# Routed FFN ahead of its first expert block: half items, the block table first, and the facts of odd tiles multiplied on GpSimd

## The chip, the cores and the metric

The kernel runs on one core of a Trainium2 chip. The metric is the device time of one execution in microseconds (us). The engines are TensorE (PE, matmuls; PEld is its weight load), VectorE (DVE), ScalarE (ACT), GpSimd (POOL) and SyncE (SP, which here only issues DMAs). Each runs its own list of instructions in order and waits on semaphores for the others. SBUF is the on-chip memory, PSUM the memory that matmuls write.

## The reference

Eight layers work on one sequence of 1024 tokens with 512 features in float32. Two of them, the sixth (L1f) and the eighth (L1g), are a routed FFN, and they alone are touched:

```
scores = sigmoid(x @ gate_w.T) + bias              # 16 experts
topk_w, topk_idx = top_k(scores, 4)                # 4 experts for each token
topk_w = topk_w / (sum(topk_w) + 1e-20)
g, u = x @ Wg[e].T, x @ Wu[e].T                    # for each expert e
out = sum over e of  cw[t, e] * (silu(g) * u) @ Wd[e].T
out = out + (silu(x @ Sg.T) * (x @ Su.T)) @ Sd.T   # the shared expert, for every token
```

The inner width is 256, for the shared expert too.

## The kernel before

`routed_ffn` computes the shared expert for all tokens, and the routed experts only for the tokens that chose them. The 4096 picks (1024 tokens, 4 each) are sorted by expert into NB = 47 blocks of 128 slots, and the blocks run one after the other.

**The head, ahead of the first block.** PE turns the normalised rows, computes the router's logits, and then the shared expert in four items. Item m is one 128-column chunk of the inner width for one half of the tokens: first its gate part (u = 0), then its up part (u = 1), 12 matmuls each. Its sums stand in PSUM pair m % 2. ACT takes the Silu of the gate part, DVE multiplies it by the up part into `z_all` (`item(m)` of DVE). PE's item m waits for DVE's item m - 2, since they use the same pair. Items and routing are interleaved in a written order: item 0, the turned scores, item 1, the ranks, items 2 and 3, `told`, the shared expert's down projection. No scheduler moves anything.

**The routing on DVE** is one long list of small instructions: score, top 8, expert indices (`hit`), `chosen`, DVE's item 0, the weights in three bf16 parts (`facts`), the places after PE's `rank`, then `slot_f`, the slot of each pick. From it come `offset_f` (slot within a block) and `at_block` (which of the 47 blocks), and for each of the 8 token tiles two products: `at_offset` (128 x 4 x 128, bf16; it lies in the tile `shared_raw`, under whose name the trace shows it) and `fact` (128 x 4 x 5 x 47 = 940 a lane, bf16). Then comes the table `block_i` of the blocks' experts, and DVE's item 1. PE sums at_offset times fact over 32 picks into `told`, and DVE makes `token` and `weight` from it: which token and weight stand in each slot.

**The down projection of the shared expert** (L1892) is 8 tiles of tokens, each 2 matmuls of float32 (4 records in the trace) into one of three PSUM banks; DVE adds each into x (L2080, `added`). It is queued on PE behind `told`.

**The blocks.** POOL gathers the rows of block b by `token` with an indirect DMA (L1754), PE turns them (`turn_block`; blocks 0 and 1 also wait for all 8 `added`), ACT and DVE split rows (L1795, L1979) and expert weights (L1788, L1972 `weights_low`) into a high and a low part, and PE multiplies (L1916 to L1918, L1939). DVE scales the result and POOL scatters it with an adding DMA. SP loads weights; its loads of experts 3 and up stand behind the stores of x after `added`, as all of SP's work is in order.

Of the kernel before, what the change touches and what calls it, by code (L numbers as in the profile page):

```python
# [6 lines left out]
ALU = mybir.AluOpType  # L7
# [1579 lines left out]
def weight_set(b):  # L1587

    return (b + 1) % 2


def pair_set(b, p):

    return (2 * (b + 1) + p) % PAIRS


def routed_ffn(nc, g, d, name, sums_dram):
    with stage(nc, name) as (sb, sem), ExitStack() as before_blocks:
# [56 lines left out]
        at_offset_ready, fact_ready, told_ready = sem("at_offset_ready"), sem("fact_ready"), sem("told_ready")  # L1655
# [20 lines left out]
        with nc.Block() as block:  # L1676
# [49 lines left out]
            def _(pool):  # L1726
# [30 lines left out]

                pool.wait_ge(g.padded, 64)
# [73 lines left out]
            def _(pe):  # L1832
# [13 lines left out]
                def item(m):  # L1846
# [4 lines left out]
                    for u in range(2):  # L1851
                        cols = slice(u * INNER + c * P, u * INNER + (c + 1) * P)
                        toks = slice(h * HALF, (h + 1) * HALF)
                        for k in range(KC):
                            mm = product(pe, g.pair[m % 2][:, u * HALF:(u + 1) * HALF], wh[:, pair_set(-1, k // 2), k % 2, cols],
                                         wl[:, pair_set(-1, k // 2), k % 2, cols], xh[:, k, toks], xl[:, k, toks], k == 0, k == KC - 1)
                    mm.then_inc(items_ready, 1)

                item(0)
# [5 lines left out]
                item(1)  # L1865
# [9 lines left out]
                item(2)  # L1875
                item(3)
                told_ps = g.bank(7)[:, 0:FACTS * NB]
                for t in range(NT):
                    pe.wait_ge(at_offset_ready, t + 1)
                    pe.wait_ge(fact_ready, t + 1)  # L1880
                    for i in range(t * TOPK, (t + 1) * TOPK):
                        mm = pe.matmul(told_ps, at_offset[:, i, :], fact[:, i, :, :], start=i == 0, stop=i == PICKS - 1)
                mm.then_inc(told_ready, 1)
                pe.wait_ge(rank_read, 1)
                pe.wait_ge(wd_loaded[weight_set(-1)], 16)
                for t in range(NT):
# [7 lines left out]
                    mm.then_inc(out_ready, 1)  # L1894

# [59 lines left out]
            def _(dve):  # L1955
# [31 lines left out]

                weights_low(-1, 0, None)
# [26 lines left out]
                with nc.allow_low_precision("zeros and ones"):  # L2015
# [30 lines left out]
                then(dve.tensor_copy(slot[:, :], slot_f[:, :]))  # L2046
                then(dve.tensor_scalar(offset[:, :], slot[:, :], P - 1, None, ALU.bitwise_and))
                then(dve.tensor_copy(offset_f[:, :], offset[:, :]))
                then(dve.tensor_tensor(first_slot[:, :], slot_f[:, :], offset_f[:, :], ALU.subtract))
                then(dve.tensor_tensor(at_block[:, :, :], first_slot[:, :].unsqueeze(2).to_broadcast([P, PICKS, NB]),  # L2050
                                       block_no[:, :].unsqueeze(1).to_broadcast([P, PICKS, NB]), ALU.is_equal))
                for t in range(NT):
                    picks, shape = slice(t * TOPK, (t + 1) * TOPK), [P, TOPK, FACTS, NB]
                    dve.tensor_tensor(at_offset[:, picks, :], offset_f[:, picks].unsqueeze(2).to_broadcast([P, TOPK, P]),
                                      in_block[:, :].unsqueeze(1).to_broadcast([P, TOPK, P]), ALU.is_equal)                        .then_inc(at_offset_ready, 1)
# [20 lines left out]
                for m in range(2, ITEMS):  # L2076
                    item(m)
# [146 lines left out]
```

## Time and profile before

| what | us |
|---|---|
| median of 3 runs | 2844.99 |
| lowest and highest run | 2842.21 and 2853.66 |
| the profiled execution, its own time | 2838.49 |
| its span from first to last instruction | 2836.7 |
| PE busy | 2586.0 (91%) |
| DVE busy | 1917.8 (68%) |
| ACT busy | 1494.7 (53%) |
| POOL busy | 823.0 (29%) |

The rows further down are of the profiled execution, and their times count from the start of its span. The granted clock of TensorE has two levels, 1.00 in a row (2.4 GHz) and 0.50 (1.2 GHz). L1g's head stands from 2461 to 2546 us, and L1f's, 768 us earlier, is alike to some tenths of a us.

### The profile page before, as it was taken

How to read it: one execution, taken by the hardware profiler on the slowest of the kernel's cores; microseconds unless marked ns; L12 is line 12 of the kernel's file. 1: busy time of each engine (PE TensorE's matmuls, PEld its weight loads, DVE VectorE, ACT ScalarE, POOL GpSimd, SP SyncE). 2: the span in 40 equal slices, each digit the busy share in tenths (PEclk: the TensorE clock that was granted, in tenths of full speed). 3: DMA queues.
4: the chain of work that ended last, by engine and by line, in shares of the span. 5: the costliest groups of instructions: out<-in, count | busy, mean ns of one | idle time of the engine just before them, and what ended most of it. 6: DMA issues, size and time to landing. Idle time of an engine off the chain costs nothing. (4 is left out here: it accounts for less than half of the span.)

```text
span 2836.7 us, 42839 instructions
## 1 busy us (share of the span) xinstructions
PE 2586.0 (91%) x14886; PEld 1777.5 (63%) x14886; DVE 1917.8 (68%) x3382; ACT 1494.7 (53%) x2528; POOL 823.0 (29%) x777
## 2 busy tenths in 40 slices
PE   7899988878999999999999987899788999868995
PEld 5444434646888888888888864566454444345663
DVE  6877724454777677777777676677578776356774
ACT  5677731314555555555555542466456777315663
POOL 1200001024344353434344320355312000003553
PEclk9899998988999999999999997999988999889998
DMA  4000000010000000000000012988810000229888
GB/s 154 1 1 2 1 18 20 18 38 23 16 23 23 16 27 16 23 23 27 16 23 20 16 35 91 325 217 202 201 58 1 1 1 2 97 75 329 202 199 206
DMA packets 68194, 197.48 MB, mean 70 GB/s; under 512 B 9040, under 2 KB 9936, under 8 KB 62608
## 3 DMA queue, kind: packets, MB, share of 16 engines
q1 hardware_dynamic: 46928, 145.44, 15.1%
q0 software_dynamic: 21056, 49.30, 9.2%
q8 instruction: 125, 2.05, 0.3%
q14 instruction: 85, 0.70, 0.1%
HBM read 154.33 MB, written 40.37 MB: 69 GB/s over the span
## 5 line engine op out<-in xcount | busy, mean ns | idle before, releaser
L1399 ACT ACTIVATE L1a_ph<-single 128x512 fp32r<-128x512 f32 (+3 forms) x384 | 174.4, 490 | 179.9 <-PE single L1486 179.2
L1540 DVE TENSOR_TENSOR L1a_pl<-single,L1a_ph 128x512 fp32r<-128x512 f32 (+3 forms) x384 | 199.2, 548 | 52.8 <-ACT L1a_ph L1399 52.1
L765 DVE TENSOR_REDUCE L0a_least<-single 128x1 f32<-128x512 f32 (+3 forms) x304 | 191.9, 660 | 57.0 <-PE single L587 30.7
L765 DVE TENSOR_REDUCE L1b_least<-single 128x1 f32<-128x512 f32 (+3 forms) x304 | 191.6, 660 | 55.7 <-PE single L587 29.9
L1556 DVE SCALAR_TENSOR_TENSOR x<-single,L1a_rinv,x 128x512 f32<-128x512 f32 x256 | 189.2, 744 | 58.5 <-PE single L1150 58.2
L1390 ACT ACTIVATE L1a_probs<-pair,L1a_least 128x128 f32<-128x128 f32 (+7 forms) x256 | 190.1, 744 | 71.6 <-DVE L1a_least L1534 70.2
L1534 DVE TENSOR_REDUCE L1a_least<-pair 128x1 f32<-128x128 f32 (+7 forms) x256 | 190.5, 749 | 43.2 <-PE pair L1475 42.6
L1367 POOL TENSOR_TENSOR L1a_swapped<-L1a_swapped,L1a_sin 128x512 f32<-128x512 f32 x80 | 129.3, 1617 | 304.5 <-ACT L1a_swapped L1431 304.5
L475 ACT ACTIVATE L0a_probsT<-pair 128x896 f32<-128x896 f32 (+2 forms) x192 | 149.0, 811 | 70.4 <-PE pair L607 47.8
L475 ACT ACTIVATE L1b_probsT<-pair 128x896 f32<-128x896 f32 (+2 forms) x192 | 149.0, 811 | 69.5 <-PE pair L607 46.9
L1486 PE MATMUL single<-ident,L1a_probs 128*128 128x128 f32 x1152 | 169.0, 274 | 1.4 <-ACT L1a_probs L1390 1.4
L1148 PE MATMUL single<-L1a_xh,L1a_wh 128*128 128x512 f32 x384 | 160.4, 418 | 6.0 <-POOL L1a_wl L1356 4.6
L1373 POOL TENSOR_TENSOR L1a_ql<-L1a_lin,L1a_qh 128x512 fp32r<-128x512 f32 x64 | 85.6, 1338 | 235.1 <-DVE L1a_qh L1578 235.1
L1149 PE MATMUL single<-L1a_xl,L1a_wh 128*128 128x512 f32 x384 | 152.3, 397 | 0.0
L1150 PE MATMUL single<-L1a_xh,L1a_wl 128*128 128x512 f32 x384 | 152.2, 396 | 0.0
L1972 DVE TENSOR_TENSOR L1g_wl<-L1g_store,L1g_wh 128x1024 fp32r<-128x1024 f32 x94 | 111.1, 1222 | 60.2 <-ACT L1g_wh L1788 59.0
L1972 DVE TENSOR_TENSOR L1f_wl<-L1f_store,L1f_wh 128x1024 fp32r<-128x1024 f32 x94 | 111.1, 1222 | 59.5 <-ACT L1f_wh L1788 58.5
L1148 PE MATMUL pair<-L1a_kh,L1a_qh 128*128 128x512 f32 (+3 forms) x384 | 140.8, 367 | 7.0 <-POOL L1a_ql L1373 5.7
L1486 PEld LDWEIGHTS single<-ident,L1a_probs 128*128 128x128 f32 x1152 | 130.0, 141 | 13.2 <-ACT L1a_probs L1390 1.7
L1149 PE MATMUL pair<-L1a_kl,L1a_qh 128*128 128x512 f32 (+3 forms) x384 | 133.0, 346 | 0.0
L1150 PE MATMUL pair<-L1a_kh,L1a_ql 128*128 128x512 f32 (+3 forms) x384 | 133.0, 346 | 0.0
L1150 PE MATMUL single<-L1a_ph,L1a_vl 128*128 128x512 f32 (+3 forms) x384 | 132.6, 345 | 0.0
(517 smaller groups left out, 7020.4 us busy)
## 6 DMA issues: line engine op xcount, KB each, us to landing
L1f_wd<-in_L1f_w SPq DMA_DIRECT2D x48, 512.0 KB, 4.4
L1g_wd<-in_L1f_w SPq DMA_DIRECT2D x48, 512.0 KB, 4.4
L1a_raw<-in_L1a_w SPq DMA_DIRECT2D x80, 256.0 KB, 2.6
L1f_store<-in_L1f_w SPq DMA_DIRECT2D x16, 1024.0 KB, 8.1
L1g_store<-in_L1f_w SPq DMA_DIRECT2D x16, 1024.0 KB, 8.3
sum<-L0a_pad_row SPq DMA_DIRECT2D x2, 2304.0 KB, 16.5
sum<-x SPq DMA_DIRECT2D x16, 256.0 KB, 3.0
x<-sum SPq DMA_DIRECT2D x16, 256.0 KB, 5.1
```

The lines of the kernel that those rows point to most:

```text
L475: act.activation(a.probsT[:, i % 2, j, 0:w], g.pair[n % 2][:, 0:w], ACT.Exp, scale=-1.0)\
L765: dve.tensor_reduce(a.least[:, part, qt, first:first + heads], g.bank(BANK16["F", kv, f])[:, 0:heads * w].rearrange("p (j k) -> p j k", j= ...
L1148: pe.matmul(out, wh, xh, start=start, stop=False)
L1149: pe.matmul(out, wh, xl, start=False, stop=False)
L1150: return pe.matmul(out, wl, xh, start=False, stop=stop)
L1390: act.activation(probs[:, u % 2, 0:n], g.pair[u % 2][:, 0:n], ACT.Exp, bias=least[:, u % 4:u % 4 + 1], scale=-1.0, accum_out=rsum[:, h % 2 ...
L1399: act.activation(p_tile(ph, u, i), turned_bank(u, i), ACT.Copy).then_inc(p_high, 1)
L1486: mm = pe.transpose(g.bank(4 + b % 2)[:, k * P:(k + 1) * P], probs[:, u % 2, kt * P:(kt + 1) * P], g.ident[:, :])
L1534: dve.tensor_reduce(least[:, u % 4:u % 4 + 1], g.pair[u % 2][:, 0:(u % NT + 1) * P], AX_X, ALU.min)\
L1540: dve.tensor_tensor(p_tile(pl, u, i), turned_bank(u, i), p_tile(ph, u, i).bitcast(F32), ALU.subtract)\
L1556: dve.scalar_tensor_tensor(out=g.x[:, t, :], in0=aux_bank(("O", h, t)), scalar=rinv[:, h % 2, t:t + 1], in1=g.x[:, t, :], op0=ALU.mult, op ...
L1972: dve.tensor_tensor(wl[:, s, :, :], src, wh[:, s, :, :].bitcast(F32), ALU.subtract).then_inc(w_split, 1)
```

## The change

PE does the items in halves (`item(m, u)`): the turned scores stand behind the first half of item 0 and not behind the whole of it, and the ranks behind the first half of item 1. The down projection (`shared_down`) is cut in three: tiles 0 to 2 ahead of `told`, tiles 3 to 5 behind `told`'s tiles 5, 6 and 7, and tiles 6 and 7 at the end. DVE does item 1 and the table ahead of `slot`, items 2 and 3 between the tiles' products, and the adds of tiles 0 to 2 among them too; its first two `weights_low` move in between the last adds. The `fact` products of tiles 1, 3, 5 and 7 are made by POOL, in the same shape, with a semaphore of their own.

```diff
@@ POOL
+                pool.wait_ge(at_block_ready, 1)
+                for t in range(1, NT, 2):
+                    picks, shape = slice(t * TOPK, (t + 1) * TOPK), [P, TOPK, FACTS, NB]
+                    pool.tensor_tensor(fact[:, picks, :, :], at_block[:, picks, :].unsqueeze(2).to_broadcast(shape),
+                                       facts[:, picks, :].unsqueeze(3).to_broadcast(shape), ALU.mult)\
+                        .then_inc(fact_ready[1], 1)
                 pool.wait_ge(g.padded, 64)
@@ PE
-                item(0)
+                item(0, 0)
                 for t in range(NT):
...
                 mm.then_inc(score_turned, 1)
-                item(1)
+                item(0, 1)
+                item(1, 0)
...
                 mm.then_inc(rank_ready, 1)
-                item(2)
-                item(3)
+                item(1, 1)
+                for m in range(2, ITEMS):
+                    for u in range(2):
+                        item(m, u)
...
+                for t in range(EARLY):
+                    shared_down(t)
+                told_ps = g.bank(7)[:, 0:FACTS * NB]
+                for t in range(NT):
+                    pe.wait_ge(at_offset_ready, t + 1)
+                    pe.wait_ge(fact_ready[t % 2], t // 2 + 1)
+                    for i in range(t * TOPK, (t + 1) * TOPK):
+                        mm = pe.matmul(told_ps, at_offset[:, i, :], fact[:, i, :, :], start=i == 0, stop=i == PICKS - 1)
+                    if t == NT - 1:
+                        mm.then_inc(told_ready, 1)
+                    if t >= NT - EARLY:
+                        shared_down(t - NT + 2 * EARLY)
+                for t in range(2 * EARLY, NT):
+                    shared_down(t)
@@ DVE
+                item(1)
...
-                then(dve.tensor_tensor(at_block[:, :, :], first_slot[:, :].unsqueeze(2).to_broadcast([P, PICKS, NB]),
-                                       block_no[:, :].unsqueeze(1).to_broadcast([P, PICKS, NB]), ALU.is_equal))
+                dve.tensor_tensor(at_block[:, :, :], first_slot[:, :].unsqueeze(2).to_broadcast([P, PICKS, NB]),
+                                  block_no[:, :].unsqueeze(1).to_broadcast([P, PICKS, NB]), ALU.is_equal)\
+                    .then_inc(at_block_ready, 1)
+                dve.wait_ge(at_block_ready, 1)
+                for t in range(NT):
...
+                    if t % 2 == 0:
+                        dve.tensor_tensor(fact[:, picks, :, :], at_block[:, picks, :].unsqueeze(2).to_broadcast(shape),
+                                          facts[:, picks, :].unsqueeze(3).to_broadcast(shape), ALU.mult)\
+                            .then_inc(fact_ready[0], 1)
+                    if t in (0, 2):
+                        item(2 + t // 2)
+                    if NT - 1 - EARLY <= t < NT - 1:
+                        add_shared(t - NT + 1 + EARLY)
...
-                for m in range(2, ITEMS):
-                    item(m)
-                for t in range(NT):
-                    dve.wait_ge(out_ready, t + 1)
-                    dve.tensor_tensor(g.x[:, t, :], g.bank(4 + t % 3), g.x[:, t, :], ALU.add).then_inc(added, 1)
+                dve.wait_ge(table_ready, 1)
+                experts = [expert_of(b) for b in range(2)]
+                for t in range(EARLY, NT - 2):
+                    add_shared(t)
+                for i in range(2):
+                    weights_low(0, i, experts[0])
+                    add_shared(NT - 2 + i)
...
-                weights_low(0, 0, experts[0])
-                weights_low(0, 1, experts[0])
```

The order of DVE's instructions before, from the slots' sum to the table (`shared_raw` is at_offset; the pair of rows L2054 and L2056 stands eight times):

```order
L2045 TENSOR_REDUCE L1f_slot_f<-L1f_part 128x32
L2046 CAST L1f_slot<-L1f_slot_f 128x32
L2047 TENSOR_SCALAR L1f_offset<-L1f_slot 128x32
L2048 CAST L1f_offset_f<-L1f_offset 128x32
L2049 TENSOR_TENSOR L1f_first_slot<-L1f_slot_f,L1f_offset_f 128x32
L2050 TENSOR_TENSOR L1f_at_block<-L1f_first_slot,L1f_block_no 128x1504
L2054 TENSOR_TENSOR L1f_shared_raw<-L1f_offset_f,L1f_in_block 128x512
L2056 TENSOR_TENSOR L1f_fact<-L1f_at_block,L1f_facts 128x940
```

and behind the last of the eight pairs, the table and item 1:

```order
L2054 TENSOR_TENSOR L1f_shared_raw<-L1f_offset_f,L1f_in_block 128x512
L2056 TENSOR_TENSOR L1f_fact<-L1f_at_block,L1f_facts 128x940
L2059 SCALAR_TENSOR_TENSOR L1f_begun<-L1f_start,L1f_block_no 128x752
L2062 TENSOR_REDUCE L1f_block_e<-L1f_begun 128x47
L2063 TENSOR_SCALAR L1f_block_e<-L1f_block_e 128x47
L2064 CAST L1f_block_i<-L1f_block_e 128x47
L1985 TENSOR_TENSOR L1f_z_all<-L1f_gate,pair 128x512
```

DVE's instructions after, behind the slots' sum, item 1 and the table (L2005 is `item`, L2010 an add into x, L2088 at_offset, L2091 fact):

```order
L2082 TENSOR_TENSOR L1f_at_block<-L1f_first_slot,L1f_block_no 128x1504
L2088 TENSOR_TENSOR L1f_shared_raw<-L1f_offset_f,L1f_in_block 128x512
L2091 TENSOR_TENSOR L1f_fact<-L1f_at_block,L1f_facts 128x940
L2005 TENSOR_TENSOR L1f_z_all<-L1f_gate,pair 128x512
L2088 TENSOR_TENSOR L1f_shared_raw<-L1f_offset_f,L1f_in_block 128x512 x2
L2091 TENSOR_TENSOR L1f_fact<-L1f_at_block,L1f_facts 128x940
L2005 TENSOR_TENSOR L1f_z_all<-L1f_gate,pair 128x512
L2088 TENSOR_TENSOR L1f_shared_raw<-L1f_offset_f,L1f_in_block 128x512 x2
L2091 TENSOR_TENSOR L1f_fact<-L1f_at_block,L1f_facts 128x940
L2010 TENSOR_TENSOR x<-single,x 128x512
L2088 TENSOR_TENSOR L1f_shared_raw<-L1f_offset_f,L1f_in_block 128x512
L2010 TENSOR_TENSOR x<-single,x 128x512
```

Four facts are gone from DVE, and items and adds stand between what is left. PE before, behind the last matmul of item 3 (L1882 is told, L1892 the down projection, L1903 the turned rows of blocks 0 and 1):

```order
L1149 MATMUL pair<-L1f_xl,L1f_wh 128x512
L1150 MATMUL pair<-L1f_xh,L1f_wl 128x512
L1882 MATMUL single<-L1f_fact,L1f_shared_raw 128x235 x32
L1892 MATMUL single<-L1f_wd,L1f_z_all 128x512 x16
L1903 MATMUL single<-ident,L1f_xn 128x128 x8
```

and after (L1897 is the down projection, L1908 told, L1923 the turned rows):

```order
L1150 MATMUL pair<-L1f_xh,L1f_wl 128x512
L1897 MATMUL single<-L1f_wd,L1f_z_all 128x512 x6
L1908 MATMUL single<-L1f_fact,L1f_shared_raw 128x235 x24
L1897 MATMUL single<-L1f_wd,L1f_z_all 128x512 x2
L1908 MATMUL single<-L1f_fact,L1f_shared_raw 128x235 x4
L1897 MATMUL single<-L1f_wd,L1f_z_all 128x512 x2
L1908 MATMUL single<-L1f_fact,L1f_shared_raw 128x235 x4
L1897 MATMUL single<-L1f_wd,L1f_z_all 128x512 x6
L1923 MATMUL single<-ident,L1f_xn 128x128 x8
```

Ten of the 16 matmuls of the down projection now stand ahead of the last piece of told.

## Rows read from the trace of the kernel before

**Rows 1.** Waits from 1709 to 1802 us (L1f), one row.

```profile
PE pair L1148 <- DVE L1f_z_all L1985: 17.8, 1, 17.8
```

**Rows 2.** Timeline of PE in L1g's head: start, us, instruction, idle before.

```profile
2484.83 0.40 PE L1148 MATMUL pair<-L1g_xh,L1g_wh 128*128 128x512 f32 x1
...
2490.44 0.67 PE L1863 MATMUL single<-ident,L1g_sigT 16*128 16x16 f32 x8
...
2520.55 0.77 PE L1148 MATMUL pair<-L1g_xh,L1g_wh 128*128 128x512 f32 x1 [17.77 <-DVE L1g_z_all L1985]
...
2528.30 3.48 PE L1882 MATMUL single<-L1g_fact,L1g_shared_raw 128*128 128x235 bf16 x32
2531.62 13.90 PE L1892 MATMUL single<-L1g_wd,L1g_z_all 128*128 128x512 f32 x32
2546.40 1.06 PE L1903 MATMUL single<-ident,L1g_xn 128*128 128x128 f32 x8 [0.88 <-DVE x L2080]
2550.54 0.79 PE L1916 MATMUL pair<-L1g_wh,L1g_bh 128*128 128x512 f32 x1 [3.08 <-DVE L1g_bl L1979]
```

**Rows 3.** Timeline of DVE in L1g's head, the same columns.

```profile
2491.14 0.29 DVE L2001 TENSOR_TENSOR L1g_score<-single,L1g_gb 128x128 f32<-128x128 f32 x1 [9.00 <-PE single L1863]
...
2502.50 1.72 DVE L2050 TENSOR_TENSOR L1g_at_block<-L1g_first_slot,L1g_block_no 128x1504 bf16<-128x1504 f32 x1
2504.26 0.69 DVE L2054 TENSOR_TENSOR L1g_shared_raw<-L1g_offset_f,L1g_in_block 128x512 bf16<-128x512 bf16 x1
2504.87 1.13 DVE L2056 TENSOR_TENSOR L1g_fact<-L1g_at_block,L1g_facts 128x940 bf16<-128x940 bf16 x1
...
2517.47 0.93 DVE L2059 SCALAR_TENSOR_TENSOR L1g_begun<-L1g_start,L1g_block_no 128x752 f32<-128x752 f32 x1
...
2519.73 0.68 DVE L1985 TENSOR_TENSOR L1g_z_all<-L1g_gate,pair 128x512 f32<-128x512 f32 x1
2531.82 0.40 DVE L2067 COPY L1g_told<-single 128x235 f32<-128x235 f32 x1 [11.41 <-PE single L1882]
...
2533.57 0.21 DVE L2075 TENSOR_TENSOR L1g_weight<-L1g_weight,L1g_told 128x47 f32<-128x47 f32 x1
...
2547.52 2.36 DVE L1972 TENSOR_TENSOR L1g_wl<-L1g_store,L1g_wh 128x1024 fp32r<-128x1024 f32 x2 [1.27 <-issue]
```

**Rows 4.** Timeline of ACT, the first block's rows.

```profile
2547.06 0.60 ACT L1795 ACTIVATE L1g_bh<-single 128x512 fp32r<-128x512 f32 x1 [15.36 <-PE single L1903]
```

**Rows 5.** Timeline of POOL: the first gather is issued.

```profile
2534.28 1.02 POOL L1754 DMA_INDIRECT L1g_xn<-rows,L1g_token  x1 [70.56 <-DVE L1g_token L2073]
```

**Rows 6.** DMA issues from 2534.2 to 2535.5 us: count, us to landing.

```profile
L1g_xn<-rows,L1g_token POOLq DMA_INDIRECT x1, 3.6
```

**Rows 7.** Busy us by stretch: PE, PEld, DVE, ACT, POOL, granted clock, DMA share, GB/s.

```profile
2504.70:2520.50 15.80, 0.00 (x0) 0.00 (x0) 15.60 (x21) 0.00 (x0) 0.00 (x0) 0.50 0.00 0
...
2550.50:2555.90 5.40, 5.36 (x13) 4.09 (x14) 2.77 (x3) 1.06 (x1) 0.21 (x1) 0.50 1.01 416
```

**Rows 8.** Timeline of POOL and of DVE around 764 us (attention, L1a).

```profile
762.90 1.29 POOL L1356 TENSOR_TENSOR L1a_wl<-L1a_raw,L1a_wh 128x512 fp32r<-128x512 f32 x1
764.15 1.75 POOL L1367 TENSOR_TENSOR L1a_swapped<-L1a_swapped,L1a_sin 128x512 f32<-128x512 f32 x1
...
764.67 1.78 DVE L1574 TENSOR_TENSOR L1a_lin<-L1a_lin,L1a_swapped 128x512 f32<-128x512 f32 x1
```

**Rows 9.** Two DVE lines, whole trace: count, ns min/median/max, first and last start.

```profile
L1574 DVE TENSOR_TENSOR L1a_lin<-L1a_lin,L1a_swapped x80: 675/681/1782, 649.3 to 1660.7; 128x512 f32<-128x512 f32 x80
...
L1540 DVE TENSOR_TENSOR L1a_pl<-single,L1a_ph x384: 272/617/692, 667.7 to 1680.8; 128x512 fp32r<-128x512 f32 x128, 128x128 fp32r<-128x128 f32 x32, 128x384 fp32r<-128x384 f32 x32
```

**Rows 10.** Timeline of POOL around 56 us: its operand `stack` is bf16.

```profile
56.08 1.40 POOL L412 TENSOR_TENSOR L0a_rest<-L0a_rc,L0a_stack 128x640 f32<-128x640 f32 x1 [6.68 <-ACT L0a_stack L493]
```

**Rows 11.** POOL's groups by shape: count, busy us, mean ns, idle before.

```profile
L435 POOL TENSOR_TENSOR L1b_parts<-L1b_most_rest,L1b_parts 128x16 bf16<-128x16 f32 x16 | 4.3, 271 | 1.3
```

**Rows 12.** Busy us by stretch, as rows 7, of the early blocks.

```profile
2562.00:2625.00 63.00, 55.38 (x232) 36.90 (x232) 42.08 (x53) 35.15 (x53) 29.09 (x21) 1.00 0.98 319
```

More of the change, by code:

```diff
@@ L1850, in item @@
                         pe.wait_ge(z_ready, m - 1)
[L1851 to L1857, printed above, removed]
-                item(0)
+                    cols = slice(u * INNER + c * P, u * INNER + (c + 1) * P)
+                    toks = slice(h * HALF, (h + 1) * HALF)
+                    for k in range(KC):
+                        mm = product(pe, g.pair[m % 2][:, u * HALF:(u + 1) * HALF], wh[:, pair_set(-1, k // 2), k % 2, cols],
+                                     wl[:, pair_set(-1, k // 2), k % 2, cols], xh[:, k, toks], xl[:, k, toks], k == 0, k == KC - 1)
+                    if u:
+                        mm.then_inc(items_ready, 1)
+                item(0, 0)
                 for t in range(NT):
@@ L1874, in _, with shared_down @@
                 mm.then_inc(rank_ready, 1)
-                item(2)
-                item(3)
-                told_ps = g.bank(7)[:, 0:FACTS * NB]
-                for t in range(NT):
[L1879 to L1886, printed above, removed]
+                item(1, 1)
+                for m in range(2, ITEMS):
+                    for u in range(2):
+                        item(m, u)
+                def shared_down(t):
+                    if t == 0:
+                        pe.wait_ge(rank_read, 1)
+                        pe.wait_ge(wd_loaded[weight_set(-1)], 16)
                     if t % BLK == 0:
@@ L2045, in _ @@
                 then(dve.tensor_reduce(slot_f[:, :], part[:, :, :, :].rearrange("p t k e -> p (t k) e"), AX_X, ALU.add))
[L2046 to L2049, printed above, removed]
-                then(dve.tensor_tensor(at_block[:, :, :], first_slot[:, :].unsqueeze(2).to_broadcast([P, PICKS, NB]),
-                                       block_no[:, :].unsqueeze(1).to_broadcast([P, PICKS, NB]), ALU.is_equal))
[L2052 to L2055, printed above, removed]
-                    dve.tensor_tensor(fact[:, picks, :, :], at_block[:, picks, :].unsqueeze(2).to_broadcast(shape),
-                                      facts[:, picks, :].unsqueeze(3).to_broadcast(shape), ALU.mult).then_inc(fact_ready, 1)
+                item(1)
                 many = [P, NB, NE]
@@ L2087, in block_out @@
                         .then_inc(y_ready, 1)
-                dve.wait_ge(table_ready, 1)
-                experts = [expert_of(b) for b in range(2)]
-                weights_low(0, 0, experts[0])
-                weights_low(0, 1, experts[0])
                 block_low(0)
```

17 lines of the change are left out of this document (13 added, 4 removed).

## The prediction

> **What bounds the kernel now.** The change touches only the head of the two routed FFNs, so I read that stretch, not the page's shares. In the timeline of PE first: behind item 2 PE stands still for 17.77 us, until DVE's item 1 [rows 2]; the waits show the same 17.8 us in L1f [rows 1]. Then DVE's timeline: in all of that time it works without a break, mostly on eight pairs of at_offset and fact, (2517.47 - 2504.26) / 8 = 1.65 us a pair, 0.61 for at_offset and 1.04 for fact [rows 3]. So DVE's list is the bound, and PE's dense work (items, down projection) stands behind a wait for it. From told's copy on DVE to the turning of block 0 it is another 2546.40 - 2531.82 = 14.6 us, in which PE works through the down projection, 13.90 / 8 = 1.74 us a tile [rows 2, 3]. What ends the head is the last add into x, not the gather: that one is issued at 2534.28 and lands 3.6 us later, 8.5 us ahead of its use [rows 5, 6]. Everything after (47 blocks) is a pipeline that starts at 2546.40, so what the head saves should arrive at the end once for each FFN, if the blocks' start moves with their loads.
>
> **The change, in L1g's times.** (1) *The turned scores earlier.* Two halves take 2490.44 - 2484.83 = 5.6 us, so the scores are turned 2.8 us earlier [rows 2], and DVE's list from L2001 on with them. PE's ranks move by the same, and each gate part is ready before DVE asks for it. (2) *Item 1 and the table ahead of the slots* add 0.6 (one item of 0.68 that overlaps the next) and 2519.73 - 2517.47 = 2.3 us to DVE ahead of at_block. Together at_block starts at 2502.50 - 2.8 + 0.6 + 2.3 = 2502.6 and ends at 2504.3, when it does now [rows 3]. Nothing is won there for DVE; but PE now has its z_all and goes on: 8 halves of 2.8 from 2484.83, plus 1.0 for scores and ranks, end at 2508.2, and three tiles of the down projection at 2513.4, in place of an idle engine.
>
> (3) *Four facts on POOL.* What one costs there no row shows. The nearest: 128x640 with one bf16 operand takes 1.40 us, 2.19 ns an element [rows 10]; 128x512 of float32 takes 1.29, 2.5 ns [rows 8]. For 940 elements that is 2.06 or 2.4 us. I take 2.06, as both operands are bf16. Bounds: not below DVE's 1.04 [rows 3], and, if each of its 20 rows of 47 were priced as an instruction of its own, 20 x 0.27 more [rows 11], 7.4 us. Against that upper end speaks rows 10: those operands too stand in short rows in the code (40 rows of 16), and the whole took 1.40.
>
> (4) *Do POOL and DVE run side by side?* By the rows they don't when both read two operands in SBUF. At 764 us POOL's product started 0.5 us ahead of DVE's sum, and DVE's took 1.78 us where the median of 80 is 0.68; POOL's own took 1.75 where its neighbour took 1.29 [rows 8, 9]. They alternate, each waiting for the other's whole instruction. DVE's L1540, which reads PSUM and one SBUF tile, is never over 0.692 in 384 times, with the same POOL at work [rows 9]: so items and adds into x aren't held, at_offset and fact are.
>
> The Trainium skill says this as a rule (SBUF — State Buffer, "Who interferes with whom"): a VectorE instruction with two SBUF inputs and a GpSimd instruction that reads SBUF exclude each other for the whole instruction, and one with a single SBUF input is free. It speaks against this change, and the trace agrees with it, 1.78 against 0.68 us. By it the sum is 22 us of gain, without it 39.
>
> With alternation from 2504.3: at_offset 0, POOL's four facts between it and fact 0, at_offset 1, at_offset 2 (0.6 + 1.0 + 0.6 + 0.6), in all 2.9 + 4 x 2.06 = 11.1 us, to 2515.4. Item 2 hides in POOL's time. Then DVE alone: three facts, five at_offsets, item 3 and three adds, 3.1 + 5.4 = 8.5 us, to 2523.9. Fact 6 is ready at 2522.7, and behind it PE does told's tile 6 (3.48 / 32 x 4 = 0.4) and the fifth down projection tile, to 2524.9, then told's last tile: told at 2525.4 instead of 2531.8, 6.4 us earlier.
>
> (5) *From told to block 0.* DVE's told to weight is 1.96, the two register loads 1.27, then three adds, weights_low (2.36 / 2 = 1.18), an add, weights_low, an add: 5 x 0.6 + 2.4. Sum 8.6 us, against 14.6 now [rows 2, 3]: 6.0 us earlier. PE's last two tiles (3.5) lie beside it, and the gather too (2.5 from told to its issue, 1.1 of which is POOL's, and 3.6 to land: 6.1 [rows 3, 5, 6]). SP issues the stores of x and the experts' loads after the same adds, so they move along.
>
> (6) *The clock.* Between 2514.2 and 2520.9 PE has only four pieces of told, 0.4 us each, while DVE is late with fact 2. Now the clock is at 0.50 from within 1.9 us of PE's stopping, and it falls again in the 3.08 us before the first block [rows 2, 7]. I take it that it falls here too, and that two down projection tiles run at the half clock, 1.7 more each: 3.4 us given back. This is the term that I am least sure of; its bounds are 0 and 3.4.
>
> (7) *The first block's split.* Its row split on DVE now stands behind two weights_low, which start at 2547.52 and take 2.36; ACT is done at 2547.66 [rows 3, 4]. With them done beforehand gate_up starts 2.1 us sooner after the turning. Bounds 0 (the gathers of blocks 3 and on then meet the experts' loads; DMA is 98% busy from 2562 to 2625 [rows 12]) and 2.1; I take 2.1, since DVE is what PE waits for there [rows 2].
>
> For one FFN 6.4 + 6.0 - 3.4 + 2.1 = 11.1 us, for two 22.2. Against the profiled execution's own 2838.5 that is 2816.3. The median of the runs shown is 6.5 us above that execution, so I forecast 2822.8, call it 2823.
>
> **The rivals.** *POOL costs nothing* (no exclusion with bf16 operands, or POOL always in DVE's gaps). DVE's loop is then 12.0 us and ends at 2516.3, PE never starves: told follows at 2520.2, block 0 at 2528.8, 17.6 us earlier, with 2.1 19.7, for two 39: 2806. Against it is [rows 8, 9]; for it, that no row has bf16 on both engines at once.
>
> *POOL's product is slow.* Each us more delays told by 4, since all four stand between DVE's products: at 3.5 us an FFN keeps 11.1 - 5.8 = 5.3, the kernel 10.6, 2834, which can't be told from no change (0.5% is 14 us, about what a measurement of this kernel can tell). For it: the inner stride-0 operand and rows of 47, which no row has.
>
> *Slower.* The same mechanism at its upper end, 7.4 us: told is 21.4 us later than in my sum, an FFN loses 10.3 us, 2866. Nothing is left of the gain at 2.06 + 11.1 / 4 = 4.8 us, and it is slower by over 0.5% from 6.6 us.
>
> *The blocks swallow it.* With DMA at 98% in the early blocks [rows 12] the start could be limited by the experts' loads rather than by PE. But those loads are issued after the same adds. It would keep (7) and some of (5) back: 8 us an FFN or less, 2829 to 2835. And the change doesn't fully do what it says anyway: PE's long wait for DVE is moved behind the items and shortened (to about 7 us, in pieces), not removed.
>
> **How the numbers follow.** My forecast, with the clock lost or kept (2816 to 2825): 0.55. POOL free: 0.12. Slow product, about 3 to 4.5 us: 0.17. Swallowed in part: 0.11. Slower: 0.05. The range is 2803 to 2836: it takes in the free POOL at its lower end and a product of 3.5 us or a swallowed part at its upper, and leaves out 0.15. The forecast's own range is 2814 to 2828. Faster by over 0.5%: all of the first two, and some of the third and fourth, 0.77. Within 0.5%: 0.18. Slower by more: 0.05.
>
> **What would show it.** PE's 17.8 us wait for z_all gone and the items without a break to about 2508 (L1g). POOL's fact at 2.1 us by itself and up to 3 where DVE holds the port; DVE's at_offset 1 and 2 lasting 2 us longer than 0.69, and the next ones 0.69. Told's copy on DVE near 2526 to 2528, against 2531.82; the turning of block 0 near 2535 to 2538; the granted clock at 0.50 once between 2515 and 2530. gate_up of block 0 about 2 us after the turning, not 4.1. The blocks' length, 282 us from 2546.4 to the end, should stay or fall by 2. I am wrong if at_offset isn't held, if POOL's fact is over 3 us, or if the blocks' stretch grows by what the head lost.

## The result: 1.1% faster, and the profile after

The changed kernel takes 2818.41 us (median of four executions, 2815.95 to 2820.56). The kernel before, on the same chip, takes 2849.32 (four, 2842.21 to 2854.78). The ratio is 0.9893, with a 95% interval of 0.9865 to 0.9921. The profiled execution takes 2815.95, with a span of 2814.2, against 2838.49 and 2836.7: 22.5 us less.

Where do the 22.5 us lie? L1f begins at 1690.89 instead of 1693.21, so 2.3 us were gained before it, in stages that the change doesn't touch. That part is no gain of the change: over all the profiles of this document that start lies anywhere between 1688.6 and 1693.2. From L1f's start to L1g's start it is 758.3 instead of 768.3, from there to the end 365.0 instead of 375.2. Each FFN is about 10 us shorter.

Times in a head are best counted from the first matmul of item 0, as the two kernels reach it at different times:

| L1f / L1g, us behind item 0 | before | after |
|---|---|---|
| last matmul of the items | 43.8 / 43.6 | 23.4 / 23.4 |
| told's copy on DVE | 47.1 / 47.0 | 40.4 / 40.3 |
| turning of block 0 | 61.7 / 61.6 | 49.2 / 48.8 |
| gate_up of block 0 | 65.5 / 65.7 | 51.3 / 50.9 |
| end of the last block's matmuls | 322.5 / 323.2 | 312.5 / 313.0 |

Timeline of PE in L1g's head, after (start, us, instruction, idle before and what ended it):

```profile
2472.41 0.39 PE L1148 MATMUL pair<-L1g_xh,L1g_wh 128*128 128x512 f32 x1
2475.26 0.67 PE L1870 MATMUL single<-ident,L1g_sigT 16*128 16x16 f32 x8
...
2495.69 5.31 PE L1897 MATMUL single<-L1g_wd,L1g_z_all 128*128 128x512 f32 x12
2500.84 0.99 PE L1908 MATMUL single<-L1g_fact,L1g_shared_raw 128*128 128x235 bf16 x8
2502.39 0.57 PE L1908 MATMUL single<-L1g_fact,L1g_shared_raw 128*128 128x235 bf16 x4 [0.56 <-DVE L1g_fact L2091]
...
2505.24 0.57 PE L1908 MATMUL single<-L1g_fact,L1g_shared_raw 128*128 128x235 bf16 x4 [1.15 <-DVE L1g_fact L2091]
...
2507.11 2.99 PE L1897 MATMUL single<-L1g_wd,L1g_z_all 128*128 128x512 f32 x4
...
2510.35 1.89 PE L1897 MATMUL single<-L1g_wd,L1g_z_all 128*128 128x512 f32 x4
...
2516.47 3.70 PE L1897 MATMUL single<-L1g_wd,L1g_z_all 128*128 128x512 f32 x8 [2.10 <-DVE x L2010]
2521.22 1.07 PE L1923 MATMUL single<-ident,L1g_xn 128*128 128x128 f32 x8 [1.05 <-DVE x L2010]
2523.27 0.50 PE L1936 MATMUL pair<-L1g_wh,L1g_bh 128*128 128x512 f32 x1 [0.98 <-DVE L1g_bl L1999]
```

The wait of 17.8 us for `z_all` [rows 1, 2] is gone. The items and three down projection tiles run without a break to 2501, and what is left of the wait stands in short pieces of 0.54 to 1.15 us between the tiles of told, 2.8 us in all. The wait of 2.10 us ahead of the last two down projection tiles is another one: they wait for DVE's add, which frees one of the three banks. The scores are turned 2475.26 - 2472.41 = 2.85 us behind item 0, where it was 5.61 [rows 2].

Timeline of DVE, the same stretch, after:

```profile
2490.21 1.73 DVE L2082 TENSOR_TENSOR L1g_at_block<-L1g_first_slot,L1g_block_no 128x1504 bf16<-128x1504 f32 x1
2491.97 0.69 DVE L2088 TENSOR_TENSOR L1g_shared_raw<-L1g_offset_f,L1g_in_block 128x512 bf16<-128x512 bf16 x1
2492.58 2.71 DVE L2091 TENSOR_TENSOR L1g_fact<-L1g_at_block,L1g_facts 128x940 bf16<-128x940 bf16 x1
2495.20 0.68 DVE L2005 TENSOR_TENSOR L1g_z_all<-L1g_gate,pair 128x512 f32<-128x512 f32 x1
2495.80 3.82 DVE L2088 TENSOR_TENSOR L1g_shared_raw<-L1g_offset_f,L1g_in_block 128x512 bf16<-128x512 bf16 x2
2499.55 2.69 DVE L2091 TENSOR_TENSOR L1g_fact<-L1g_at_block,L1g_facts 128x940 bf16<-128x940 bf16 x1
...
2503.97 1.12 DVE L2091 TENSOR_TENSOR L1g_fact<-L1g_at_block,L1g_facts 128x940 bf16<-128x940 bf16 x1
...
2509.06 0.68 DVE L2088 TENSOR_TENSOR L1g_shared_raw<-L1g_offset_f,L1g_in_block 128x512 bf16<-128x512 bf16 x1
2512.68 0.40 DVE L2099 COPY L1g_told<-single 128x235 f32<-128x235 f32 x1 [2.94 <-PE single L1908]
```

and POOL's first two products in L1g, then its four products in L1f and L1g (ns: lowest, median, highest; first and last start):

```profile
2492.09 2.20 POOL L1762 TENSOR_TENSOR L1g_fact<-L1g_at_block,L1g_facts 128x940 bf16<-128x940 bf16 x1 [40.74 <-DVE L1g_at_block L2082]
2494.25 2.65 POOL L1762 TENSOR_TENSOR L1g_fact<-L1g_at_block,L1g_facts 128x940 bf16<-128x940 bf16 x1
...
L1762 POOL TENSOR_TENSOR L1f_fact<-L1f_at_block,L1f_facts x4: 2197/2209/2652, 1734.0 to 1741.0; 128x940 bf16<-128x940 bf16 x4
L1762 POOL TENSOR_TENSOR L1g_fact<-L1g_at_block,L1g_facts x4: 2197/2207/2654, 2492.1 to 2499.0; 128x940 bf16<-128x940 bf16 x4
```

POOL's product takes 2.20 us. While POOL works, until 2501.25, two facts of DVE take 2.7 us, where one alone takes 1.1, and two at_offsets take 3.82, where two alone take 1.3. The item between them, which reads PSUM and one tile in SBUF, keeps its 0.68. At_block starts at 2490.21, 17.80 us behind item 0; before, it was 17.67 [rows 2, 3]. What the earlier scores won, item 1 and the table have used up.

Busy us of PE, PEld, DVE, ACT and POOL by stretch, granted clock, DMA share, GB/s, after:

```profile
2472.40:2495.90 23.50, 23.50 (x115) 18.98 (x114) 18.90 (x60) 3.67 (x6) 3.81 (x2) 1.00 0.08 23
...
2505.90:2509.30 3.40, 2.95 (x7) 1.66 (x8) 3.40 (x6) 0.00 (x0) 0.00 (x0) 0.50 0.41 154
2509.30:2521.20 11.90, 8.77 (x26) 3.60 (x25) 7.55 (x16) 0.00 (x0) 3.80 (x3) 1.00 0.39 125
2521.20:2543.40 22.20, 18.02 (x82) 12.88 (x82) 15.27 (x19) 13.60 (x20) 7.34 (x6) 1.00 1.01 381
2543.40:2550.30 6.90, 5.33 (x12) 3.06 (x13) 1.44 (x2) 0.94 (x2) 0.00 (x0) 0.51 0.79 274
```

In the head the clock is at its lower level (1.2 GHz) for 3.4 us, and one down projection tile takes 2.99 us for 1.89. The first block now runs at 2.4 GHz, where before it ran at 1.2 [rows 7]. But the half clock is back from 2543.4 on, inside a wait of 3.58 us for a gather:

```profile
2544.97 1.11 PE L1923 MATMUL single<-ident,L1g_xn 128*128 128x128 f32 x4 [3.58 <-DMA L1g_xn<-rows,L1g_token]
```

The waits of PE for gathers in the 126 us from the turning on, after (us in total, times, longest):

```profile
PE single L1923 <- DMA L1g_xn<-rows,L1g_token: 11.1, 8, 3.6
```

and before:

```profile
PE single L1903 <- DMA L1g_xn<-rows,L1g_token: 8.2, 9, 2.5
```

The DMA share is 1.01 in the 22 us up to 2543.4. In L1f the same waits are 10.1 us after (longest 3.5) and 8.2 before (longest 1.8).

### The profile page after: what moved, and what is told of

The parts are those of the page before. It is cut to its first block and busy times, and to the rows that moved or that the text cites. A ratio compares the mean times of both kernels' runs of the same rounds, so it can differ in the third digit from the quotient of the medians.

```text
span 2814.2 us, 42845 instructions
## 1 busy us (share of the span) xinstructions
PE 2584.7 (92%) x14886; PEld 1772.7 (63%) x14886; DVE 1918.9 (68%) x3374; ACT 1493.7 (53%) x2528; POOL 842.5 (30%) x785
## 5 line engine op out<-in xcount | busy, mean ns | idle before, releaser
L1540 DVE TENSOR_TENSOR L1a_pl<-single,L1a_ph 128x512 fp32r<-128x512 f32 (+3 forms) x384 | 199.5, 549 | 52.6 <-ACT L1a_ph L1399 52.0
L1486 PEld LDWEIGHTS single<-ident,L1a_probs 128*128 128x128 f32 x1152 | 130.0, 141 | 13.2 <-ACT L1a_probs L1390 1.7
## 6 DMA issues: line engine op xcount, KB each, us to landing
L1a_raw<-in_L1a_w SPq DMA_DIRECT2D x80, 256.0 KB, 2.6
sum<-x SPq DMA_DIRECT2D x16, 256.0 KB
x<-sum SPq DMA_DIRECT2D x16, 256.0 KB, 4.9
```

Of the source, the lines that this page charges most:

```text
L1486: mm = pe.transpose(g.bank(4 + b % 2)[:, k * P:(k + 1) * P], probs[:, u % 2, kt * P:(kt + 1) * P], g.ident[:, :])
L1540: dve.tensor_tensor(p_tile(pl, u, i), turned_bank(u, i), p_tile(ph, u, i).bitcast(F32), ALU.subtract)\
```

## The experiments

There were eleven runs: eight new kernels, two of them twice, and the changed one again. Head times are again us behind item 0, L1f / L1g; "blocks" is from the turning of block 0 to the end of the last block's matmuls, in L1g before 2806.07 + 1.98 - 2546.40 = 261.7. Ratios are to the kernel before on the same chip. Four kernels were executed only once. Their times of the head can be read all the same, since these repeat where the clock does the same: the changed kernel's two profiles agree in told and in the turning within 0.1 us. The blocks' length doesn't repeat; it moves by up to 3 us between profiles of one kernel.

**All facts on DVE, in the changed kernel** (`e1_facts_dve`). Does POOL's help pay?

```diff
-                for t in range(1, NT, 2):
-                    pool.tensor_tensor(fact[:, picks, :, :], ...)
...
-                    if t % 2 == 0:
-                        dve.tensor_tensor(fact[:, picks, :, :], ...).then_inc(fact_ready[0], 1)
+                    dve.tensor_tensor(fact[:, picks, :, :], ...).then_inc(fact_ready[t % 2], 1)
```

> The changed kernel with all eight facts on VectorE; nothing is left to GpSimd, all else of the change stays. Theory (the engines exclude each other at the SBUF port): in the changed kernel four facts on GpSimd held VectorE's list for 4 x 2.2 us and saved it 4 x 1.05, so taking them back should bring told's copy 4 to 4.5 us nearer to the first item's start (from 40.3 to about 36) and the turning of block 0 from 48.8 to about 44.7 in each FFN. If all of it arrived the kernel would be 8 us shorter than the changed one, 0.3%; if the blocks' stretch swallows it as it did with part of the head's gain, 0 to 4 us. Rival (the offload pays, the long VectorE rows have another cause): told's copy comes 2 to 4 us later than in the changed kernel.

Measured: 2813.39 (four), ratio 0.9889 (0.9866 to 0.9912) to the 2843.64 beside it. Timeline of DVE, then of PE:

```profile
2508.86 0.40 DVE L2092 COPY L1g_told<-single 128x235 f32<-128x235 f32 x1 [0.76 <-PE single L1902]
...
2516.33 0.69 DVE L2004 TENSOR_TENSOR x<-single,x 128x512 f32<-128x512 f32 x1 [1.42 <-PE single L1891]
```

```profile
2508.66 1.89 PE L1891 MATMUL single<-L1g_wd,L1g_z_all 128*128 128x512 f32 x4
...
2512.64 5.37 PE L1891 MATMUL single<-L1g_wd,L1g_z_all 128*128 128x512 f32 x8 [2.09 <-DVE x L2004]
2518.90 1.06 PE L1917 MATMUL single<-ident,L1g_xn 128*128 128x128 f32 x8 [0.89 <-DVE x L2004]
```

and the window of the last two down projection tiles' first part, columns as above:

```profile
2512.60:2516.00 3.40, 3.36 (x4) 1.52 (x5) 2.31 (x3) 0.00 (x0) 2.78 (x2) 0.50 0.72 211
```

Item 0 starts at 2472.24, so told is at 36.6 (36.6 in L1f too): 3.7 us earlier than with POOL. The turning is at 2518.90 - 2472.24 = 46.7 (L1f 47.1), only 2.1 earlier: the first of the last two down projection tiles now runs at the half clock (5.37 us for 3.70 for both), DVE waits 1.42 us for it, and PE sets what follows told. So both gains fell short of what was expected (4 to 4.5 us at told, 4.1 at the turning), but their sign is clear: the products on POOL don't pay, and the gain of the change comes from its other parts.

**Only the odd facts on POOL, in the kernel before** (`e2_before_pool`): the other half of the same question.

```diff
+                pool.wait_ge(at_block_ready, 1)
+                for t in range(1, NT, 2):
+                    pool.tensor_tensor(fact[:, picks, :, :], ...).then_inc(fact_ready[1], 1)
...
-                    dve.tensor_tensor(fact[:, picks, :, :], ...).then_inc(fact_ready, 1)
+                    if t % 2 == 0:
+                        dve.tensor_tensor(fact[:, picks, :, :], ...).then_inc(fact_ready[0], 1)
```

> The kernel before with the facts of odd tiles on GpSimd and nothing else of the change. Theory (exclusion): VectorE's stretch from the first at_offset to the table grows from 13.2 us to 4 x 2.2 for GpSimd's facts and 9.0 for what VectorE keeps, 17.8, so told and all behind it come 4.6 us later in each FFN, the kernel 9 us longer (0.3%). Rival (they run side by side): the stretch falls to 9.0 us and the kernel is 8 us shorter.

Measured: 2851.27 (ten), ratio 1.0023 (1.0011 to 1.0035). Timeline of DVE, then of POOL:

```profile
2507.82 0.69 DVE L2063 TENSOR_TENSOR L1g_shared_raw<-L1g_offset_f,L1g_in_block 128x512 bf16<-128x512 bf16 x1
2508.43 2.70 DVE L2066 TENSOR_TENSOR L1g_fact<-L1g_at_block,L1g_facts 128x940 bf16<-128x940 bf16 x1
2511.05 4.42 DVE L2063 TENSOR_TENSOR L1g_shared_raw<-L1g_offset_f,L1g_in_block 128x512 bf16<-128x512 bf16 x2
2515.39 2.69 DVE L2066 TENSOR_TENSOR L1g_fact<-L1g_at_block,L1g_facts 128x940 bf16<-128x940 bf16 x1
...
2523.10 0.93 DVE L2070 SCALAR_TENSOR_TENSOR L1g_begun<-L1g_start,L1g_block_no 128x752 f32<-128x752 f32 x1
```

```profile
2507.94 9.15 POOL L1762 TENSOR_TENSOR L1g_fact<-L1g_at_block,L1g_facts 128x940 bf16<-128x940 bf16 x4 [40.82 <-DVE L1g_at_block L2057]
```

DVE's loop takes 2523.10 - 2507.82 = 15.3 us, against 2517.47 - 2504.26 = 13.2 before [rows 3], with four products fewer in it. Told comes 1.9 / 2.8 us later. That is the direction of exclusion, but not its expected size, a loop of 17.8 us and told 4.6 us later. Its own work is 8 x 0.61 + 4 x 1.04 = 9.0, so it stands still for 6.3 us. If each POOL product of 2.20 us excluded DVE from start to end it would be 8.8. So about 6.3 / 4 = 1.6 us of each are exclusive, and about 0.6 are not. Two more readings agree: at_offset 0 (2507.82 to 2508.51) lies for 0.57 us beside POOL's first product, and neither is longer for it (0.69, and 2.20 in the changed kernel, where they overlap by the same 0.57); and in the changed kernel POOL's second product had to let 1.04 us of DVE's fact pass, yet took only 2.65 - 2.20 = 0.45 longer. The Trainium skill (SBUF — State Buffer, "Who interferes with whom") says that whoever issues first has the shared ports for the whole instruction; the runs agree in the exclusion, and differ by these 0.6 us of an instruction as the profile shows it. Whether they are work that needs no port or a start noted too early, no run shows.

**Only the half items, in the kernel before** (`e6_half_only`):

```diff
-                item(0)
+                item(0, 0)
                 ...
-                item(1)
+                item(0, 1)
+                item(1, 0)
```

> The kernel before with the items in halves alone (scores turned behind the first half of item 0, ranks behind the first half of item 1); VectorE's list, the down projection and the facts are as before. Theory (VectorE's list is the bound, and it starts with the turned scores): told's copy comes 2.8 us sooner, 44.2 in place of 47.0 us behind the first item, and the turning of block 0 at 58.8 in place of 61.6; the kernel gains up to 5.6 us less what the blocks swallow. Rival (PE's wait for the second item's product sets told, whatever VectorE starts with): told's copy stays at 47.

Measured: 2839.36 (ten), ratio 0.9983 (0.9968 to 0.9998). Timeline of DVE, item 0 at 2484.56:

```profile
2528.05 0.40 DVE L2070 COPY L1g_told<-single 128x235 f32<-128x235 f32 x1 [10.65 <-PE single L1885]
```

Told is at 43.5 (44.0 in L1f) and the turning at 58.6 / 58.1, in both 3 to 3.5 us earlier. Told was expected 2.8 us earlier, so this part is worth what it should be. It is by itself a real but small gain.

**Whole items, in the changed kernel** (`e7_whole_items`): the turned scores stand behind `item(0, 1)`, the ranks behind `item(1, 1)`.

```diff
                 item(0, 0)
+                item(0, 1)
...
-                item(0, 1)
                 item(1, 0)
+                item(1, 1)
...
-                item(1, 1)
```

> The changed kernel with PE's items whole again (scores turned behind all of item 0, ranks behind all of item 1); all else of the change stays. Theory (the parts add): told's copy 2.8 us later than in the changed kernel, 43.1 in place of 40.3 us behind the first item, turning of block 0 at 51.6 in place of 48.8. Rival (the other parts hide it): less than 1 us.

Measured: 2822.68 (one execution). Told is at 2520.62 - 2477.23 = 43.4 (L1f 43.5), 3.1 later, and the turning at 53.8 / 53.5, 4.6 later: about 2 us later than expected. Timeline of DVE:

```profile
2520.62 0.40 DVE L2099 COPY L1g_told<-single 128x235 f32<-128x235 f32 x1 [3.32 <-PE single L1908]
```

Windows of the same kernel, columns as above:

```profile
2510.80:2517.60 6.80, 5.61 (x16) 2.68 (x17) 6.50 (x10) 0.00 (x0) 0.00 (x0) 0.50 0.22 82
2524.40:2527.90 3.50, 3.50 (x4) 1.50 (x5) 2.28 (x3) 0.00 (x0) 2.79 (x2) 0.51 0.79 223
```

The clock is at its lower level in two places. In the second stands the first of the last two down projection tiles, and the two take 5.40 us instead of 3.70; that is most of what lies between expected and measured. Half items are worth 4.6 us at the turning of the changed kernel.

**Told ahead of the down projection, in the changed kernel** (`e8_told_first`): all 8 tiles and all adds stand behind told.

```diff
-                for t in range(EARLY):
-                    shared_down(t)
...
-                    if t >= NT - EARLY:
-                        shared_down(t - NT + 2 * EARLY)
-                for t in range(2 * EARLY, NT):
+                for t in range(NT):
                     shared_down(t)
```

> The changed kernel with the down projection behind told as before (all eight tiles, and all adds behind told); items, table, halves and the facts on GpSimd as changed. Theory (of the 6.1 us between told and block 0 the early tiles are the cause): told's copy comes about 2 us sooner (38.3), since three adds are out of VectorE's list, but the turning of block 0 follows 14.6 us or more behind it, at 53 to 55 us in place of 48.8. Rival (VectorE, not PE, sets the time from told to block 0): turning of block 0 at 49 or sooner.

Measured: 2821.67 (one execution). Timeline of PE, item 0 at 2477.51:

```profile
2507.47 0.94 PE L1906 MATMUL single<-L1g_fact,L1g_shared_raw 128*128 128x235 bf16 x4 [4.29 <-DVE L1g_fact L2087]
...
2514.09 14.10 PE L1897 MATMUL single<-L1g_wd,L1g_z_all 128*128 128x512 f32 x32
2529.11 1.06 PE L1919 MATMUL single<-ident,L1g_xn 128*128 128x128 f32 x8 [0.91 <-DVE x L2006]
```

Told comes at 36.8, 3.5 us earlier than in the changed kernel (2 were expected), but then the turning waits for 14.1 us of down projection and is at 52.6 / 51.6: 3.4 / 2.8 later, about 1 us less than expected. The early tiles delay told and yet are worth about 3 us.

**Are the blocks limited by the loads of weights?** (`e3_after_thin`, `e4_before_thin`) In the two profiles compared, the changed kernel loses, behind gate_up of block 0, 4.2 to 4.6 us of what its head had won. In both kernels the loads of the down weights were cut to a corner of 64 KB for all blocks from the second on, so these two don't compute the FFN.

```diff
                 def down_weights(b, ...):
+                    if b >= 1:
+                        sp.dma_start(wd[:, weight_set(b), 0:1, 0:P], src[:, 0:1, 0:P]).then_inc(...)
+                        return
```

> The changed kernel, but of the down weights of blocks 1 and on only a corner is loaded (64 KB in place of 512 KB a block), so that those blocks multiply by stale down weights; all instructions but those loads are unchanged. Theory (the blocks' early stretch is limited by what the DMA engines must move, so it swallowed the earlier and warmer start of block 0): PE's wait of 3.5 us for a gather some 24 us behind the turning of block 0 goes, with it the fall of the clock behind it, and turning to last down matmul falls from 264 us to under 257. Rival (the loss comes from another wait, the gathers' own latency or the scatters): that stretch stays at 262 or more.

> The kernel before with the same cut of the down weights' loads (64 KB in place of 512 KB a block, so those blocks multiply by stale down weights). Theory: its stretch from the turning of block 0 to the last down matmul falls too, from 261.5 us to 253 to 258, but stays 4 to 5 us longer than that of the changed kernel with the same cut, since there block 0 has its split done (2.1 us) and a full clock (2.7 us). Rival (nothing was swallowed, the head's gain never reached the blocks): both kernels with the cut differ by under 2 us in that stretch.

Measured, one execution each: 2800.52 and 2829.99. Blocks: 254.3 / 257.3 after, 257.3 / 259.1 before. Uncut the changed kernel's were 2.4 / 2.5 us longer than the other's, cut they are 3.0 / 1.8 shorter. Expected were 4 to 5 shorter by the theory and under 2 by its rival, so the result lies between them. In the profile behind the 1.8 the first block of L1g ran at 1.2 GHz in the changed kernel too (0.80 us for its first matmul), so that the warm start was missing there. Waits of PE for gathers in the same 126 us, after and then before, both cut:

```profile
PE single L1926 <- DMA L1g_xn<-rows,L1g_token: 6.8, 6, 1.6
```

```profile
PE single L1906 <- DMA L1g_xn<-rows,L1g_token: 6.3, 5, 2.3
```

So the changed kernel's waits fall from 11.1 to 6.8 us and its longest from 3.6 to 1.6, the other's only from 8.2 to 6.3. The direction is that of the theory, but one execution each can't carry the size: with their loads whole and in their old place, the blocks behind the old head took 260.8 to 268.0 us (mean of six 264.0), those behind a new head 261.0 to 267.5 (mean of twelve 263.2).

The profile of `e3_after_thin` also shows what a stretch at the half clock costs. Its head is that of the changed kernel, but in L1f the clock stayed at 2.4 GHz between the pieces of told. Timeline of DVE, item 0 at 1712.78:

```profile
1751.81 0.40 DVE L2102 COPY L1f_told<-single 128x235 f32<-128x235 f32 x1 [1.69 <-PE single L1911]
```

Told is at 39.0 there, 1.4 us earlier than the 40.4 of the changed kernel.

**The loads moved to where DMA is idle** (`e5_early_loads`), a version that follows from it: all facts on DVE, and the loads of experts 4 to 7 issued as soon as the last item is done.

```diff
+                sp.wait_ge(items_ready, ITEMS)
+                for e in range(EARLY + 1, EARLY + 5):
+                    stored(e)
...
-                        for e in range(EARLY, EARLY + 2):
-                            stored(e)
-                    if b + EARLY + 2 < NE:
-                        stored(b + EARLY + 2)
+                        stored(EARLY)
+                    if b + EARLY + 5 < NE:
+                        stored(b + EARLY + 5)
```

> The changed kernel with all facts on VectorE (as in the earlier run of that kind), and with the weights of experts 4 to 7 loaded as soon as PE's last item is done (23 us behind the first item's start) in place of behind the adds; expert 3's load keeps its place and the experts from 8 on move up. Nothing is left out. Theory (the blocks' early stretch is limited by what must be moved): 4 of 13 MB go in a stretch where the DMA engines stand idle, so PE's waits for gathers in the first 80 us of the blocks (some 12 us in all) mostly go, and turning of block 0 to the last down matmul falls from 262 to 264.5 us to about 255; the kernel is 14 to 18 us shorter than with the facts on VectorE alone, near 0.983 of the kernel before. Rival (the gathers' own latency and the scatters make the waits): the stretch stays over 260 and the kernel at 0.989. Second rival: the loads delay the first gathers or the stores of x, and block 0 starts later.

Measured: 2804.57 (five), ratio 0.9859 (0.9834 to 0.9883). DMA issues of this kernel from 2491 to 2494 us (count, KB each, us to landing):

```profile
L1g_store<-in_L1f_w SPq DMA_DIRECT2D x4, 1024.0 KB, 7.9
```

The head is that of `e1_facts_dve` to 0.1 us, and the blocks take 260.6 / 256.0 instead of 264.5 / 262.2: 3.9 and 6.2 shorter. Expected were about 255 us for the blocks and a kernel 14 to 18 us shorter than `e1_facts_dve`; it is 8.8 shorter, on another chip. So the loads account for about half of what was laid to them.

**Three versions on one chip**, since the differences are small: the changed kernel, all facts on DVE, and the early loads on top.

> The changed kernel as it is, beside the next two on one chip, so that the three can be compared with each other. Expected: near 0.989 of the kernel before, as measured the first time.

> The changed kernel with all facts on VectorE, once more. Theory (the four facts on GpSimd cost 2.1 us at the turning of block 0 in each FFN): 4 us less than the changed kernel beside it, 0.15%, near what can be measured. Rival (the blocks swallow all of it): no difference.

> The same with the weights of experts 4 to 7 loaded behind PE's last item, once more. Theory (the blocks' early stretch is limited by the transfers): 8 us less than the one beside it without the early loads, 12 less than the changed kernel (0.4%). Rival (the first time was chance): no difference between these two.

| | median (range), us | ratio to before (2842.78) | turning | blocks |
|---|---|---|---|---|
| e9, changed | 2820.18 (2815.01 to 2821.62) | 0.9910 (0.9893 to 0.9926) | 49.2 / 48.9 | 261.4 / 263.9 |
| e10, facts on DVE | 2809.42 (2806.46 to 2817.91) | 0.9875 (0.9856 to 0.9894) | 47.1 / 46.7 | 267.5 / 263.6 |
| e11, early loads | 2803.35 (2800.99 to 2803.52) | 0.9850 (0.9830 to 0.9871) | 47.1 / 46.7 | 262.1 / 258.2 |

Facts on DVE are 10.8 us better than the change. The head shows 2 x 2.1 = 4.2 of it. The profile of e10 is its slowest execution (2817.91, with long blocks), so it can't show the rest. The 10.8 is on the high side: with the earlier executions of the same kernels added, the medians are 2819.4 (ten) and 2811.7 (nine), 7.7 us apart. Against that slowest profile the early loads shorten the blocks by 5.4 / 5.4; the medians are 6.1 apart, and with the earlier executions added 8.1 (2803.5, nine). e11 is the best version and 39.4 us ahead of the kernel before.

No run takes the table and item 1 back behind the products, the two items and three adds out from between them, or the first `weights_low` back behind the last add, so what these parts are worth by themselves is read from the traces alone.

## Why the prediction was right, and which terms were off

The forecast was 2823 with faster as the likely side; measured is 2818.4, in the forecast's own range. Against the profiled execution the sum said 22.2 us and 22.5 were measured, of which 2.3 lie outside the FFNs. In an FFN it is 10.1 for 11.1, but made of terms whose errors cancel: gate_up of block 0 came 14.3 / 14.9 us earlier, over 3 us more than the 11.1 of the sum, and the blocks gave 4.2 / 4.6 back, which the sum had at nothing. That the number fits so well is in part luck; the mechanism of the head was right.

- **(1) and (2), the list ahead of at_block: right.** The scores came 2.8 us earlier, at_block stayed within 0.13 us, and the items ended 23.4 us behind item 0 as worked out (2508.2 - 2484.83). That PE's wait is moved and shortened, not removed, held too, but 17.8 us became 2.8 in pieces, not about 7.
- **(3), a product on POOL at 2.06 us: 2.20 measured,** 7% more. At 2.34 ns an element it lies midway between the two neighbours of 2.19 and 2.5 ns [rows 8, 10], so that both operands are bf16 was no ground for the lower one. The upper end of 7.4 us, and with it the slower rival and the slow product, is excluded.
- **(4), exclusion: right in kind, too strong in size.** The step that was too strong is "each waiting for the other's whole instruction". It put POOL's part at 4 x 2.06; by the runs DVE loses 4 x 1.6. So DVE's list ended 37.3 us behind item 0 instead of 39.1, 1.8 earlier, which is 4 x (2.06 - 1.6). The rival that POOL costs nothing fell: two facts of DVE take 2.7 us.
- **Told 6.4 us earlier: 6.7 measured.** The 1.8 us were mostly not passed on. At 2507.11 PE runs the fourth tile of the down projection at the half clock, so DVE is done at 2509.7 and idles 2.94 us for told: here PE, not DVE, is last. Where that tile ran at full clock (L1f of `e3_after_thin`) told was at 39.0 and DVE idled 1.69.
- **(5), told to block 0: 8.5 us for 8.6** (2521.22 - 2512.68), 8.8 in L1f.
- **(6), the clock: mis-sized.** I took 3.4 us to be given back, two tiles at the half clock; it was one tile, 2.99 - 1.89 = 1.1, and a piece of told beside it, together 1.4 at told (40.4 against 39.0), and it lies in front of told, inside the 6.7. So terms (4) to (6), forecast as 9.0, gave 12.5 / 12.8. The clock did fall behind the pieces of told, for 3.4 us, but earlier than I took, when most of the down projection was already done. In `e1_facts_dve` and `e7_whole_items` the first of the last two tiles did run at the half clock, for 1.7 us more.
- **(7), the first block's split: right.** From turning to gate_up 2.04 us for 3.85 / 4.14. The first block also ran at full clock, which no term had: its 5.4 us at half clock [rows 7] held some 2.7 us. That is not sure to happen: in the changed kernel's other profile (`e9_changed_again`) the first matmul of L1g's first block takes 0.79 us, not 0.50.
- **"The blocks' stretch should stay or fall by 2": missed in the profiles compared, not settled beyond them.** gate_up of block 0 came 14.3 / 14.9 us earlier, and 10.1 / 10.2 were left at the end. What the swallowed rival described happened there in part. The warm clock's 2.7 us went again with the half-clock stretch at 2543.4, where PE's 5.33 busy us would have been 2.7 at full clock; it begins inside the wait of 3.58 us for a gather, and PE waits 11.1 - 8.2 = 2.9 us longer for gathers in all (1.9 in L1f). I had held that the loads move along with the start. They do, but so do the gathers, and in the first 22 us of the blocks DMA is full. The cut loads and the early loads both shorten this stretch, which shows that the loads matter in it. That they make up just this difference between before and after is argued only, and over all executions the difference is smaller: the 43 of the kernel before have a median of 2843.9, the ten of the changed one 2819.4, 24.5 us less. So of the 29.1 us by which the two gate_ups together came earlier, 4.6 are missing, not the 8.8 of the profiles, and by the mean of the profiles the blocks are no longer than before (263.2 for 264.0, from the turning on).
- **The medians** are 30.9 us apart in the first comparison, 22.6 on the chip of the last three (2842.78 against 2820.18), and 24.5 over all executions. The kernel before varies by 15 us, so the first gap is no sign of a missing term. Against the 24.5 the sum of 22.2 is 2 us short.

What I didn't ask in the prediction is whether the part on POOL helps at all. It could be had from my own numbers: with exclusion, four products on DVE are 4 x 1.04 = 4.2 us, and on POOL they held it for 4 x 2.06. The undo-one-part runs gave 2 us a head lost by it, and half items and the order of the down projection as what pays, each with 3 to 4.6 us at the turning (they overlap and don't add up to the 12.7).

## What to carry to other kernels

Before a product is moved from VectorE to GpSimd, compare not the two engines' loads but the time that each version holds what they share: here 1.6 us a product on GpSimd against 1.04 on VectorE, a loss while both engines had work. When a head is shortened, look at what the first 50 us behind it wait for; with DMA full there, moving loads to where it stands idle (8% in the head) was worth 6 to 9 us here, about as much as taking the products off GpSimd (8 to 11 us by the medians, of which the heads show 4). And when dense work is spread to fill waits, note where in it the clock falls, as a stretch of 3.4 us at half clock cost 1.4 us ahead of told and 1.7 behind it.

## What was not expected of the hardware

- GpSimd's bf16 product of 128x940 with two broadcast operands takes 2.20 us, 2.34 ns an element, though its innermost rows are 47 long and one operand repeats within them. About the first 0.6 us of it, as the profile shows it, excluded nothing: VectorE's at_offset ran beside it at 0.69 us.
- PE stopped only for pieces of 0.5 to 1.2 us between tiles of told in the head, and the clock was at 1.2 GHz from 2505.90 to 2509.30 all the same. With the same waits in L1f of `e3_after_thin` it stayed at 2.4 GHz. In the changed kernel it was back at 2.4 GHz while PE waited 2.10 us ahead of the last two down projection tiles (2514.4 to 2516.5), and those ran at full speed, 1.85 us each. With the facts on DVE the same two tiles stand behind a wait of 2.09 us and take 5.37 us, the first of them at 1.2 GHz. What tells the two apart was not tried: it stays open.
